# Two attention loops issued by offsets, the value sum moved from VectorE to GpSimd, and unread products in six pauses of TensorE

## The reference, cut to what matters

```python
x = x + attn_a(ln(x))     # 32 query heads, 8 key heads of 64, rope, causal softmax over 1024 tokens
x = x + ffn(ln(x))        # a router picks 128 of 1024 tokens; attention (16 heads of 128) and MLP on these
x = x + attn_b(ln(x))     # 16 heads of 128 with biases, causal softmax over 1024 tokens
x = x + ffn(ln(x))        # the same chosen-token layer again
```

```python
logits = jnp.where(causal, einsum('bhqd,bhkd->bhqk', q, k) * scale, -inf)
out = einsum('bhqk,bhkd->bhqd', softmax(logits), v)
return out.transpose(0, 2, 1, 3).reshape(b, s, H * HD) @ Wo.T
```

## Time and profile before

| what | value |
|---|---|
| three runs, median (lowest to highest) | 1779.75 us (1777.93 to 1782.86) |
| profiled execution, its own time | 1778.83 us |
| its span, first to last instruction | 1777.6 us |
| TensorE busy | 1526.5 us, 86% of the span |
| VectorE, ScalarE, GpSimd busy | 67%, 54%, 39% |
| mean granted TensorE clock | 0.93 of full |

### The profile page before, as it was taken

One profiled execution on the slowest core, in us unless ns is written; L12 is line 12 of the kernel. 1 busy time (PEld: TensorE's weight loads), 2 busy tenths in 40 slices (PEclk: granted clock), 3 DMA queues, 4 the chain that ended last, 5 costly groups with the idle time before them and its releaser, 6 DMA issues.

```text
span 1777.6 us, 24716 instructions
## 1 busy us (share of the span) xinstructions
PE 1526.5 (86%) x8394; PEld 1259.6 (71%) x8394; DVE 1194.1 (67%) x2825; ACT 966.2 (54%) x2119; POOL 694.4 (39%) x777
## 2 busy tenths in 40 slices
PE   6889897989888887677699999999996777787898
PEld 4768686777777776367488888888884664565676
DVE  4788788888888886453466666666665536577445
ACT  2676767677776776122265555555551235344654
POOL 4446363645545443310242433243322204871223
PEclk8899999999999999787899999999997888898899
DMA  1000000000000000500100000000005004000000
GB/s 65 10 10 7 10 16 1 16 1 16 1 7 1 7 1 1 237 1 0 42 19 13 25 17 20 13 25 19 7 1 237 1 1 166 0 0 1 1 1 24
DMA packets 13936, 46.23 MB, mean 26 GB/s; under 512 B 3058, under 2 KB 3058, under 8 KB 11380
## 3 DMA queue, kind: packets, MB, share of 16 engines
q1 hardware_dynamic: 13812, 44.66, 7.0%
HBM read 43.60 MB, written 1.05 MB: 25 GB/s over the span
## 4 chain that ended last, share of the span: by engine, by line
PE 59%; DVE 18%; ACT 12%; issue 7%; POOL 3%; DMA 0%; DVEq 0%; ACTq 0%; POOLq 0%; SPq 0%
PE ps L140 22%; PE ps L343 13%; PE ps L332 6%; ACT a_prob L362 4%; DVE a_pT_lo L403 4%; PE ps L1651 2%; PE ps L1645 2%; ACT a_pT_hi L395 2%; DVE a_prob L354 2%; ACT a_q L579 1%; PE ps L1155 1%; PE ps L1088 1%; PE ps L213 1%; PE ps L1647 1%; DVE f_r L1283 1%
## 5 line engine op out<-in xcount | busy, mean ns | idle before, releaser
L378 POOL TENSOR_SCALAR a_prob<-a_prob,a_rowinv 128x128 f32<-128x128 f32 (+7 forms) x256 | 192.2, 752 | 307.8 <-DVE a_rowinv L371 307.7
L362 ACT ACTIVATE a_prob<-a_prob,a_negmax 128x128 f32<-128x128 f32 (+7 forms) x256 | 199.0, 777 | 73.8 <-DVE a_negmax L354 72.8
L403 DVE TENSOR_TENSOR a_pT_lo<-ps,a_pT_hi 128x512 fp32r<-128x512 f32 (+3 forms) x384 | 200.9, 551 | 24.4 <-ACT a_pT_hi L395 22.0
L332 PE MATMUL ps<-ident,a_prob 128*128 128x128 f32 x1152 | 177.4, 283 | 41.3 <-DVE a_pT_lo L403 37.0
L378 POOL TENSOR_SCALAR b_prob<-b_prob,b_rowinv 128x128 f32<-128x128 f32 (+7 forms) x128 | 96.2, 751 | 260.6 <-DVE b_rowinv L371 260.6
L354 DVE CUSTOM_DVE_ANT_0 a_prob<-ps,a_mask 128x128 f32<-128x128 f32 (+7 forms) x256 | 191.5, 748 | 2.4 <-PE ps L140 2.3
L395 ACT ACTIVATE a_pT_hi<-ps 128x512 fp32r<-128x512 f32 (+3 forms) x384 | 173.6, 487 | 32.9 <-PE ps L332 29.7
L332 PEld LDWEIGHTS ps<-ident,a_prob 128*128 128x128 f32 x1152 | 135.6, 144 | 65.2 <-POOL a_prob L378 31.7
L140 PE MATMUL ps<-a_k_hi,a_q 128*128 128x512 f32 (+3 forms) x384 | 156.0, 406 | 4.1 <-DVE a_k_lo L628 1.4
L343 PE MATMUL ps<-a_pT_hi,a_v 128*128 128x512 f32 (+3 forms) x384 | 132.3, 352 | 19.5 <-DVE a_pT_lo L403 19.0
L140 PE MATMUL ps<-a_k_lo,a_q 128*128 128x512 f32 (+3 forms) x384 | 131.6, 355 | 0.0
(11 more groups left out here) (436 smaller groups left out, 4187.3 us busy)
## 6 DMA issues: line engine op xcount, KB each, us to landing
f_wq<-in_f_wq SPq DMA_DIRECT2D x2, 2048.0 KB, 9.9
f_wo<-in_f_wo SPq DMA_DIRECT2D x2, 2048.0 KB, 18.6
b_w_raw<-in_b_qk SPq DMA_DIRECT2D x16, 256.0 KB, 2.7
a_w_raw<-in_a_w SPq DMA_DIRECT2D x8, 384.0 KB, 3.1
a_o_raw<-in_a_o SPq DMA_DIRECT2D x8, 256.0 KB, 2.6
f_rope<-in_f_rope SPq DMA_DIRECT2D x2, 1024.0 KB, 5.3
f_wk<-in_f_wk SPq DMA_DIRECT2D x2, 1024.0 KB, 11.7
f_wv<-in_f_wv SPq DMA_DIRECT2D x2, 1024.0 KB, 14.4
```

The lines of the kernel that those rows point to most:

```text
L332: t = pe.transpose(g.ps[:, b, j * P:j * P + P], a.prob[:, slot, (j0 + j) * P:(j0 + j + 1) * P], g.ident[:])
L362: act.activation(prob, prob, ACT.Exp, bias=a.negmax[:, slot:slot + 1], scale=-1.0, accum_out=a.rowsum[:, slot:slot + 1]).then_inc(*g.exped ...
L378: pool.tensor_scalar(prob, prob, a.rowinv[:, slot:slot + 1], 1.0, ALU.mult, ALU.mult).then_inc(*g.normed.mark(a.tag, u))
L403: dve.tensor_tensor(lo, src, fr(hi), ALU.subtract).then_inc(*g.lo.mark(a.tag, u, j0 // 4))
```

## The change

1. **Order by offsets.** Each engine's loop over steps becomes a loop over `in_turn`, which sorts all units and jobs by "unit number plus an offset of this kind" (one offset for even and one for odd units). The job tables move a few jobs by a step. For most kinds the order on the engine stays as it was. In `attn_a`, ScalarE takes the high parts of a long unit ahead of the `val` copy, and GpSimd scales a long unit one step sooner. In `attn_b`, TensorE turns the short unit right after the scores four units later, and the jobs stand behind it.
2. **The value sum.** In `attn_a` ScalarE copies both halves of a `val` product (two 64x512 copies in place of one) into `o_two`, which frees the bank; GpSimd adds the two halves, once for every pair of heads (32 adds of 128x512). VectorE's 64 adds at L636 are gone.
3. **Waits.** A transpose waits for the low parts that were in its own bank only; `out` waits for the half of the tokens that it reads; waits on weights stand at the first job of a set only; some waits that follow from others are gone.
4. **Memory.** `prob` gives 512 columns to short units and 1024 to long ones.
5. **Unread products.** In both chosen-token layers `spin_pe` issues 84, 22, 18, 40, 36 and 20 bf16 products of 256 columns in the six pauses, into a PSUM bank that nothing reads; the next write to this bank waits for them.

```diff
+def in_turn(a, units, jobs):
+    turns = [(u + late[u % 2], kind, u) for kind, late in units.items() for u in range(len(a.units))]
+    turns += [(s + late, kind, job) for s, todo in a.jobs.items() for job in todo for kind, (of, late) in jobs.items() if job[0] == of]
+    return [(kind, what) for _, kind, what in sorted(turns, key=lambda turn: turn[0])]
...
 def turn_pe(g, a, pe, u):
     pe.wait_ge(*g.normed.at(a.tag, u))
-    if u >= 2:
-        pe.wait_ge(*g.lo.at(a.tag, u - 2, 0 if i < 4 else len(parts(a.units[u - 2][2])) - 1))
     for j0, n, b in parts(i):
+        if u >= 2 and j0 <= a.units[u - 2][2]:
+            pe.wait_ge(*g.lo.at(a.tag, u - 2, j0 // 4))
...
+A_AT = {'project': [5, 6, 7, 7, 9, 10, 17, 18, 21, 22, 23, 23, 24, 25], 'val': [11, 12, 11, 12, 11, 12, 11, 12], 'out': [12, 13, 16, 16]}
+A_PE = ({'scores': (0, 0), 'turned': (3.5, 3.8)}, {'tok': ('tok', 0.1), 'turn': ('turn', 0.1), 'val': ('val', 0.1), 'out': ('out', 0.1)})
+A_ACT = ({'hi': (4.2, 3.9), 'exp': (1.3, 1.3)}, {'tok': ('tok', 0.85), 'turn': ('turn', 0.4), 'val': ('val', 1), 'o_hi': ('val', 3.1)})
+A_DVE = ({'max': (0.7, 0.7), 'invert': (2.1, 2.1), 'lo': (4.6, 4.6)}, {'tok': ('tok', 1.5), 'turn': ('turn', 1.2), 'out': ('out', 0.9)})
+A_POOL = ({'norm': (2.1, 1.25)}, {'tok': ('tok', 1.1), 'w': ('tok', 1.75), 'out': ('out', 0.65), 'val': ('val', 0.95), 'o_lo': ('val', 2.5)})
...
-        project = [5, 6, 7, 8, 9, 10, 17, 18, 21, 22, 23, 24, 25, 26]
...
-                act.activation(a.o_low[64:128], out[64:128], ACT.Copy).then_inc(*g.copied.mark(*ev))
+            for e2 in range(2):
+                t = act.activation(a.o_two[ROWS[h % 2], qb, e2], g.ps[ROWS[e2], a.side[what], :], ACT.Copy)
+            t.then_inc(*g.copied.mark(a.tag, what))
...
-                dve.wait_ge(*g.copied.at(*ev))
-                dve.tensor_tensor(a.o_sum[ROWS[h % 2], qb], out[0:64], a.o_low[64:128], ALU.add).then_inc(*g.drained.mark(*ev))
...
+            pool.wait_ge(*g.copied.at(a.tag, what))
+            pool.tensor_tensor(both[:, 0], both[:, 0], both[:, 1], ALU.add).then_inc(*g.o_sum.mark(gr, h, qb))
...
+B_AT = {'qk': [1, 1, 3, 6, 8, 8, 13, 14], 'v': [4, 5, 7, 9], 'val': [11, 12, 11, 12], 'out': [9, 10, 14, 16]}
+B_PE = ({'scores': (0, 0), 'turned': (4.25, 3.8)}, {'qk': ('qk', 0.7), 'v': ('v', 0.7), 'val': ('val', 0.7), 'out': ('out', 0.7)})
+B_ACT = ({'hi': (4.05, 3.6), 'exp': (1.3, 1.45)}, {'qk': ('qk', 0.55), 'v': ('v', 0.55), 'val': ('val', 0.55)})
...
+    spin_pe(g, f, pe, 6, 84, "beats")
     pe.wait_ge(*pool.at(tag, "beats"))
...
+    spin_pe(g, f, pe, 4, 22, "take")
...
+    spin_pe(g, f, pe, 5, 18, "h")
...
+    spin_pe(g, f, pe, 7, 40, "rope")
...
+    spin_pe(g, f, pe, 7, 36, "softmax")
...
+    spin_pe(g, f, pe, 3, 20, "h2")
...
+def spin_pe(g, f, pe, bank, times, name):
+    ones = g.ident[:].bitcast(BF16)
+    for _ in range(times):
+        t = pe.matmul(g.ps[:, bank, 0:D], ones[:, 0:P], ones, start=True, stop=True)
+    t.then_inc(*g.f_pe.mark(f.tag, "spin", name))
```

495 lines of the change are left out of this document (240 added, 255 removed).

## The result

The changed kernel takes 1756.0 us in the median of 4 runs (1749.2 to 1758.5), the kernel before 1778.8 in its 4: a ratio of 0.986, 95% interval 0.983 to 0.990. It is faster, by 23 us and not by the 60 forecast; the time lies above the range. The profiled execution is the fastest of the four, 1749.2 us.

The account below looks back on a forecast made before the run. The prediction took each first-attention head's floor as its busiest engine after the move, TensorE in most. From 1778.8 us it took 45, 2, 0 and 13 for 1718.8, said as 1719, range 1693 to 1750 for 8 in 10.

Parts of the forecast that it names:

- the first attention's term: First attention's loop: moving the value sum off VectorE gains 45 us, seven tenths of 64 if every head reached its floor.
- Its lower bound: First attention's loop: at least 1.5 us per group, 12 us, from two heads that TensorE doesn't bound.
- the ring: First attention: VectorE waits 57.9 us for ScalarE's copy, ScalarE 72.1 for the value product, TensorE's transposes 37.0 for VectorE.
- The second attention: Second attention's new order: gain taken as 0 us, bounds -3 and +5, since TensorE has 4 us idle in 446.
- The end of the first attention: Last output products: the first can run in TensorE's 4.0 us idle time; 2 us gain, bounds 0 and 4.
- The unread products: Both chosen-token layers: a warmer clock behind the pauses gains 7.2 and 5.8 us, together 13, bounds -4 and +22.
- `softmax`: Chosen-token layers' pause ahead of L1138: 1.3 us gain if warm, 1.0 taken since the clock may fall again.
- Rival E: Chosen-token layers: by the transposes' rule the `softmax` term is 0 and the time 1721; chance 0.64 together with the forecast.
- A: First attention: only the work is saved, ScalarE takes VectorE's place in the ring; loop gains 12, 1752 us; chance 0.15.
- B: First attention: all idle time goes, every head reaches TensorE's own busy time; loop gains 75, 1685 us; chance 0.10.
- C: Chosen-token layers: unread products run at half clock, 19 us late in each layer, and warm nothing; 1770 us; chance 0.05.
- D: First attention: GpSimd's new sum delays its scaling, for which TensorE's transposes wait; slower, up to 79 us, 1798; chance 0.06.

Follow-up runs that it names:

- the swaps: VectorE takes a tile's row maximum ahead of the low half four places back: on the changed kernel 1776.6 us, on the kernel before 1819.1 us.
- the longer rings: Changed kernel with the row maximum ahead of the low half, six probability slots, one rope buffer, transposes behind the scores four places on: 1810.1 us.
- e6: Changed kernel with all tables of the second attention back in the old order: 1757.4 us.
- e11: Changed kernel with the first attention back in the old order, the value sum still on GpSimd: 1766.5 us, loop 670.2 us.
- e5: Changed kernel with the value sum back on VectorE, in the new order: 1780.5 us, loop 681.2 us.

## Why the prediction was wrong

**The step that failed** is the first attention's term: "Now each head's floor is the busiest engine after the move", and from it 45 us. The loop gained 4.4. A floor by the busiest engine holds only if work can be moved in time freely; in these queues it can't. Room in an engine's total did not mean room at the place where the work was put: the moved work alone cost 11 us. Nor is work that is taken off worth its length: VectorE lost 43.8 us of sum and 58 of waiting for it, and stands 82 us more at the next instruction instead (22.0 to 104.7). The chain of the kernel before could have told it: the sum whose 43.8 us I priced made 0.7 us of it. In place of a floor the runs show a chain through the queues, and what lies on it comes through: the copies, 23.7 us of it after and 4.5 before, and GpSimd's queue in the head with projections, 64.3 us for none.

**Its lower bound failed too.** I took 12 us as sure, from VectorE's saved 1.37 us in two heads less ScalarE's 1.19 in one. That priced ScalarE's copies only where ScalarE was the busiest. The bound should have reached below zero; no reason excluded a loss.

**I named the ring and followed it wrongly.** The first part of the prediction says that VectorE's backlog stops TensorE. I then asked what is late next and answered with ScalarE in one head only. The chain shows it in the head without jobs as well: two turns of 3.7 us, and in series with them the two copies (1.1 us) and the value product (3.3 us), the rest being parts of further turns. My sum had no term for anything in series. Whether a shorter ring alone would win is open: the swaps and the longer rings closed other ways, and no run shortened it by itself. The cut of the value product, which lets the next tile's transposes in between, took 0.4 us of its 3.3.

**The second attention** was taken at 0; its order gave 4.7 us in the loop, inside my bound of 5. The 1.4 us behind the loop stay when the order is taken back (e6); the finer waits are the part of the change that is left to explain them, which is argued and not shown.

**The end of the first attention** was taken at 2 and gave 0.1: TensorE's pause ahead of the output products is 3.90 us for the 4.01 of the earlier trace rows. The longer chain seems to have taken what the finer wait gave; no run parts the two.

**The unread products** were right: 13 us forecast, 13 alone and 17 on top of the order. By pauses in the first layer, against the earlier trace rows: the first is not lengthened (9.33 and 2.60 for 11.77); `h` gives 1.6 (9.01 to 7.41; 1.2 taken); `rope` 2.5 (6.29 to 3.84; 2.5); `h2` 2.6 (two blocks in 3.65 for 6.28; 2.5); `take` 1, not 0, and it comes 1.5 us late, 1.9 said; `softmax` nothing (5.09 to 5.36; 1.0). In the second layer it gave 0.8:

```profile
797.70:801.90 4.20, 2.10 (x15) 1.39 (x14) 2.33 (x5) 4.18 (x18) 0.00 (x0) 1.00 0.00 0
...
1406.02 3.74 PE L1144 MATMUL ps<-f_probT,f_v 128*128 128x128 f32 x32
```

In both layers the unread products kept the granted clock at 1.00 through the transposes, four of which take 0.66 us where they took 1.12 at 0.50. In the first layer the clock fell half a microsecond into L1144, in the second it stayed. Over the 17 kernels that have the 36 products of this pause L1144 took 3.74 us in 24 of its 34 places and 4.8 to 5.6 in the others; in the three kernels without them it took 4.6 to 5.1 in all six. So the term of 1.0 was fair as a mean, and in the first layer of this execution it had bad luck. The Trainium skill, "TensorE: Matmul & The Clock Gate", Part 4, has it that the full clock is not granted for transposes, since they don't count as busy time in the same way. These rows differ from it: the clock was full in the transposes, and behind them it was kept more often than lost. Rival E came true in the first layer alone.

**The rivals.** A gave 1752 us, a loop gain of 12 and ScalarE in VectorE's place: nearest in time and in kind, and I gave it 0.15. B and C did not come: TensorE still idles 71 us, and the products run over in one pause only. D's time did not come, but half of what it describes did. TensorE's transposes wait for GpSimd's scaling for 21.0 us in 26 places, where it was 3.6 in 3, which was one of my signs of being wrong. What stands in GpSimd's queue there are rope sums and low-part differences, not the new sum. In e11 1.1 us of GpSimd lie on the chain and in e5 5.3, so it takes the new order and the moved work together.

## What to carry to other kernels

In a pipeline of in-order queues, do not price moved work by the busiest engine. First look how much of it lies on the chain of waits; what lies beside it can't be won directly. Then follow the ring: write down for each instruction the one ahead of it in its queue and the one that releases it, go round until the same operation of a later tile, and divide by the tiles passed; work counts where it lies in that ring or lengthens a wait in it, and a swap that opens one ring has to be followed into the next. A change of place and a change of load belong together and can each be a loss alone, so the bound of either reaches past zero.

## What the runs showed of the hardware

In the head with transposes the granted clock fell further than before, which no part of the prediction had. Three microseconds each, from the changed kernel:

```profile
264.60:267.60 3.00, 0.66 (x4) 0.42 (x4) 2.35 (x6) 2.96 (x8) 2.11 (x3) 0.81 0.00 0
267.60:270.60 3.00, 2.08 (x9) 1.89 (x9) 2.94 (x8) 2.94 (x8) 1.80 (x2) 0.50 0.00 0
270.60:273.60 3.00, 2.98 (x13) 2.88 (x14) 2.81 (x7) 2.95 (x7) 0.82 (x2) 0.50 0.00 0
273.60:276.60 3.00, 3.00 (x16) 2.90 (x15) 2.96 (x8) 1.78 (x5) 0.58 (x2) 0.50 0.00 0
```

TensorE is idle for 2.51 us at 265.3, waiting for VectorE's `a_q`, and then works for 8.1 us at the lower of its two levels, 1.2 GHz, which at the higher one would be some 4 us (an estimate by half). Over this head the clock is 0.79. Of the seven such heads with jobs of a next group, two have 0.79 and take 24.5 and 24.3 us, and five have 0.86 and take 24.1; before, six had 0.93 and one 1.00, and in e11, where the jobs keep their old steps, all have 0.93. The loop's 3360 products take TensorE 583.8 us after and 577.2 before. That the new steps of the transposes give back part of what the order gains is likely, since TensorE makes 12.9 us of this head's chain for 3.8 before; it was not tried by itself.

A one-column operation takes 0.20 us on ScalarE, 0.15 on VectorE and 0.19 on GpSimd by its own record and only 0.09, 0.07 and 0.16 in the queue, since the next begins before it ends. And the same code does not take the same time in each execution: the first norm and chosen-token stage with the unread products took 152.2 to 157.9 us over the kernels here, a spread of 5.7 us where the best single pause gave 2.6.
